# Four graph layers on one core: b2 added by DMA and bk on VectorE instead of matmuls, with a new order of work in layers 0 and 2

## The chip, the cores and the metric

The kernel runs on one core of a Trainium2 chip. The metric is the device time of one execution in microseconds, lower is better.

## The reference

The input is x, 64 graphs of 128 nodes with 256 features, and one 128 x 128 adjacency matrix per graph. Four layers follow one another, each inside a residual and a layer normalisation:

```
x = _layernorm(x + L0(x, adj, W1, b1, gamma, beta, W2, b2))   # hypergraph convolution, relu, layer norm, convolution + b2, + x
x = _layernorm(x + L1(x, adj, W_qk, W_v))                     # q k scores summed with adj, softmax over nodes, times v
x = _layernorm(x + L2(x, adj, Wv, bv, aw, ab, Wk, bk))        # attention transition T; relu(sum_k T^k x Wk[k] + bk[k])
x = _layernorm(x + L3(x, adj, w, a))                          # tanh attention, T x w
```

Layer 0 in full is `y = P norm(relu(P x W1 + b1)) W2 + b2`, with P = D^-1 H B^-1 H^T of the graph, and its result is `y + x`, so the layer normalisation sees `2 x + y`. In layer 2:

```
e = leaky_relu(sj[:, None, :] + si[:, :, None] + ab[0], negative_slope=0.2)
transition = A * exp(e); transition /= sum(transition, -1) + 1e-12
H = X Wk[0] + bk[0] + T X Wk[1] + bk[1] + T T X Wk[2] + bk[2];  return relu(H)
```

## The kernel before, in words

The 64 graphs are taken in 16 groups of four (`GP = 4`). x stays in SBUF (`K.x`, 64 KB a partition), and so does the transposed adjacency (`K.at`). Each layer has five programs, one an engine (SP, TensorE, ScalarE, VectorE, GpSimd), and each program is a function `step(g, p, has)` in which the order of the pieces is written out by hand. A step handles pieces of several groups at once: `has(-1)` means "if group g-1 exists", p is the parity of g. `over_layers` runs all steps of a layer on an engine and interleaves the last steps of one layer with the first of the next as the strings `SEAMS_*` say. Engines only meet through semaphores.

Precision is had by halves: a float32 value is split into an f16 high and an f16 low part, and `triple` makes three matmuls out of one product (L86 low x high, L87 high x low, L88 high x high).

Layer 0, per group on TensorE: `hidden` (four pieces, 1.3 us each), `spread_degrees`, `gram`, `mix_z` of the group before, `transpose_adj` and `degree` of a later group, `project` (four pieces), `mix_x`, `square_sums`. `mix_z` adds b2: a matmul of ones with `b2_parts` (L634) opens the bank, and P times zn (L635) is accumulated on it. `layer_out` on VectorE (L868) takes half of this plus x, loaded by SP into `K.x` (`load_resident`, L444). ScalarE makes relu, squares, z copies; GpSimd adds up the squares (`sum_squares`, L969), and `squares_high` (L698), `squares_low` and `square_sums` follow. During the first groups weights are prepared in parts of `K.x` and `K.at` that are not in use yet (`setup`); SP waits for them before it loads group 6.

Layer 2, per group on TensorE: `node_scores` (24 small matmuls), `project_near` (four pieces, six matmuls of 512 columns each), `spread_scores`, `project_far` (four), `walk_far` and `walk_mid` (four each, multiplications by T). `walk_mid` adds bk with a matmul of ones with `bk_parts` (L1546). ScalarE applies relu from PSUM (L1612) and VectorE adds x (L1665). The scores go: `logits` on ScalarE (L1587), leaky relu on VectorE (L1680), `exponentials` on ScalarE (L1619), `transition`, `row_sums` and `normalised` on VectorE, `T_high` and `T_low`, and two DMA transposes of T by SP.

x for a layer's matmuls has to be turned. `x_high` (ScalarE, L1114) and `x_low` (GpSimd, L1121) make halves of a group's x, and `transpose_x` (L1135, SP queue) turns them by DMA into `xT_hi` and `xT_lo`. There are two buffers of each, so the transposes of group g+2 overwrite those of group g. In layer 2 they wait for `near_ps` of group g, the fourth `project_near`:

```
if s == 0 and reused(g):
    sp.wait_ge(readers[0], upto(g - 2, readers[1], readers[1]))
sp.dma_start(F.xT[p][s][:].rearrange("p g d n -> p (g d) n"),
             F.xs[p][s].rearrange("p g d -> p (g d)"), transpose=True).then_inc(F.xT_in[p], 16)
```

and `node_scores(g+2)`, the first reader, waits for both (`transposed`).

## Time and profile before

| | |
|---|---|
| Median of 3 runs | 706.57 us (703.46 to 710.72) |
| Profiled execution, own time | 706.9 us |
| Its span | 704.9 us |
| Mean granted TensorE clock | 0.981 |
| Busy: TensorE, VectorE, ScalarE, GpSimd | 93%, 80%, 76%, 51% |
| Layer 0, 1, 2, 3, roughly | 0 to 285, to 390, to 600, to 705 us |

The span is what the profiler's records cover; the times of runs are a little longer. A line of a view names the source line, the engine, the operation and what it writes and reads. A matmul's duration contains its way through the array, so matmuls that follow each other overlap in the records: how long one holds the engine is seen from the start of the next.

### The profile page before, as it was taken

What the parts mean: (1) busy time and instruction counts of PE and PEld (TensorE: products, weight loads), DVE (VectorE), ACT (ScalarE), POOL (GpSimd) and SP (SyncE); (2) the same over time, 40 slices, a digit from 0 to 9 for tenths busy, and PEclk for the clock granted to TensorE, in tenths of its full rate; (3) what the DMA queues carried; (4) which work ended last, traced back from release to release, by engine and by line L of the source; (5) the groups of instructions that cost most, each with busy time, mean ns of one, the idle gap of its engine ahead of it and who ended that gap; (6) DMA issues with size and microseconds to landing.
All of it is one profiled execution on the core that took longest, in us unless ns stands there. A gap on an engine that the chain in (4) does not pass through costs nothing.

```text
span 704.9 us, 16982 instructions
## 1 busy us (share of the span) xinstructions
PE 652.6 (93%) x5526; PEld 469.1 (67%) x5526; DVE 560.8 (80%) x1746; ACT 538.7 (76%) x1193; POOL 358.3 (51%) x434
## 2 busy tenths in 40 slices
PE   5899999999999998989997899999989999899994
PEld 5667776777777775656664556666656766677783
DVE  4899899988888887588888668686867876688886
ACT  4768878787888878578887656777767776799996
POOL 2234455544444446466666324535335353688983
PEclk9999999999999999999999799999999999999998
DMA  9422324222222100476655133345533434377883
GB/s 280 148 74 84 98 65 131 75 77 75 76 76 76 62 16 16 94 157 134 134 133 117 44 81 78 87 87 91 92 74 78 90 77 75 61 169 175 180 189 129
DMA packets 168174, 71.50 MB, mean 101 GB/s; under 512 B 122260, under 2 KB 165654, under 8 KB 168088
## 3 DMA queue, kind: packets, MB, share of 16 engines
q1 hardware_dynamic: 166496, 70.41, 42.0%
q8 instruction: 45, 0.74, 0.4%
q14 instruction: 41, 0.34, 0.2%
q10 hardware_dynamic: 1592, 0.01, 0.1%
HBM read 28.46 MB, written 8.39 MB: 52 GB/s over the span
## 4 chain that ended last, share of the span: by engine, by line
PE 64%; DVE 10%; DMA 8%; POOL 7%; ACT 6%; issue 5%; SPq 1%; ACTq 0%; POOLq 0%; DVEq 0%
PE banks L86 17%; PE banks L88 16%; PE banks L87 16%; DMA xT_lo<-x_halves 7%; POOL x_halves L1121 4%; PE banks L635 3%; PE banks L594 3%; DVE l_st L1035 2%; ACT h_hi L683 2%; POOL l_rstd L1060 2%; PE banks L1440 1%; DVE l_pre L1312 1%; POOL l_U L1965 1%; PE banks L1546 1%; PE banks L580 1%
## 5 line engine op out<-in xcount | busy, mean ns | idle before, releaser
L1069 ACT ACTIVATE x_resident<-l_pre,l_nmr,l_rstd 128x256 f32<-128x256 f32 x256 | 141.0, 601 | 11.9 <-POOL l_nmr L1063 11.3
L969 POOL TENSOR_TENSOR hq<-hq 128x512 f32<-128x512 f32 x48 | 61.9, 1289 | 101.1 <-ACT hq L692 98.8
L1121 POOL TENSOR_TENSOR x_halves<-x_resident,x_halves 128x1024 f16<-128x1024 f32 x46 | 98.1, 2132 | 28.5 <-DVE l_pre L1312 24.1
L86 PE MATMUL banks<-Wk_lo,xT_hi 128*128 128x2 f16 (+2 forms) x384 | 95.1, 277 | 4.5 <-DMA xT_lo<-x_halves 4.5
L87 PE MATMUL banks<-Wk_hi,xT_lo 128*128 128x2 f16 (+2 forms) x384 | 96.0, 276 | 0.0
L88 PE MATMUL banks<-Wk_hi,xT_hi 128*128 128x2 f16 (+2 forms) x384 | 95.6, 275 | 0.0
L1035 DVE BATCH_NORM_STATS2 l_st<-l_pre 128x6 f32<-128x256 f32 x256 | 94.8, 414 | 0.0
L1060 POOL TENSOR_TENSOR l_rstd<-l_veps,minus_half 128x4 f32<-128x4 f32 x64 | 70.1, 1095 | 15.3 <-DVE l_veps L1049 11.9
L86 PE MATMUL banks<-W2T_lo,h_hi 128*128 128x257 f16 x256 | 70.9, 277 | 3.5 <-ACT zf L704 2.7
L1762 POOL TENSOR_TENSOR l_T_lo<-l_tf,l_T_hi 128x512 f16<-128x512 f32 x16 | 18.5, 1158 | 106.2 <-ACT l_T_hi L1606 106.2
L87 PE MATMUL banks<-W2T_hi,h_lo 128*128 128x257 f16 x256 | 70.9, 277 | 0.0
L88 PE MATMUL banks<-W2T_hi,h_hi 128*128 128x257 f16 x256 | 70.9, 277 | 0.0
L679 ACT ACTIVATE hf<-banks,b_col 128x512 f32<-128x512 f32 x64 | 43.9, 685 | 17.3 <-PE banks L88 16.9
L86 PE MATMUL banks<-xT_lo,W1T_hi 128*128 128x512 f16 x128 | 48.7, 380 | 2.9 <-DVE qkvT_lo L384 0.9
L86 PE MATMUL banks<-w_lo,xT_hi 128*128 128x1 f16 (+1 forms) x256 | 44.8, 218 | 6.1 <-DMA xT_lo<-x_halves 5.0
L86 PEld LDWEIGHTS banks<-Wk_lo,xT_hi 128*128 128x128 f16 x384 | 35.0, 98 | 21.2 <-DMA xT_lo<-x_halves 7.3
L88 PE MATMUL banks<-xT_hi,W1T_hi 128*128 128x512 f16 x128 | 48.5, 379 | 0.0
L87 PE MATMUL banks<-xT_hi,W1T_lo 128*128 128x512 f16 x128 | 48.5, 379 | 0.0
L1114 ACT ACTIVATE x_halves<-x_resident 128x1024 f16<-128x1024 f32 x46 | 48.4, 1052 | 0.0
L88 PEld LDWEIGHTS banks<-Wk_hi,xT_hi 128*128 128x128 f16 x384 | 35.4, 98 | 17.7 <-issue 1.4
L87 PE MATMUL banks<-w_hi,xT_lo 128*128 128x1 f16 (+1 forms) x256 | 45.8, 218 | 0.0
L88 PE MATMUL banks<-w_hi,xT_hi 128*128 128x1 f16 (+1 forms) x256 | 45.4, 218 | 0.0
(208 smaller groups left out, 1984.4 us busy)
## 6 DMA issues: line engine op xcount, KB each, us to landing
adj<-in_adj SPq DMA_DIRECT2D x32, 256.0 KB, 4.1
x_halves<-in_x SPq DMA_DIRECT2D x16, 512.0 KB, 3.9
x_resident<-in_x SPq DMA_DIRECT2D x16, 512.0 KB, 5.3
out<-x_resident SPq DMA_DIRECT2D x15, 512.0 KB, 3.3
l_adjT<-adjT_resident SPq DMA_DIRECT2D x16, 256.0 KB, 2.6
x_resident<-in_L_gnn_W SPq DMA_DIRECT2D x2, 512.0 KB, 5.6
x_resident<-in_L_gnn_Wk SPq DMA_DIRECT2D x1, 768.0 KB, 8.1
xT_hi<-x_halves SPq DMA_TRANSPOSE x48, 3.2
```

Source lines behind the costliest of these rows:

```text
L86: nc.tensor.matmul(out, lhs[0], rhs[1], start=start, stop=False, **kw)
L87: nc.tensor.matmul(out, lhs[1], rhs[0], start=False, stop=False, **kw)
L88: return nc.tensor.matmul(out, lhs[0], rhs[0], start=False, stop=stop, **kw)
L594: m = pe.matmul(b_mix[d][:, c], xst[p][:, j, d * 128:(d + 1) * 128], pf[p][:, c], start=True, stop=True)
L635: m = pe.matmul(o, pf[p][:, j * N:(j + 1) * N], zn[p][:, j, :], start=False, stop=True)
L679: act.activation(hf[:, h, :], b_hid[h % 2][:], ACT.Relu, bias=K.b1[:, h:h + 1], scale=1.0 / W_SCALE).then_inc(hf_ok, 1)
L969: pool.tensor_tensor(hq[:, 0, :], hq[:, 0, :], hq[:, h, :], ALU.add).then_inc(hqs_ok, 1)
L1035: dve.bn_stats(L.st[p][:, j, :], L.pre[p][:, j, :]).then_inc(L.st_ok, 1)
L1060: pool.tensor_tensor(L.rstd[p][:], L.veps[p][:], K.minus_half[:], ALU.pow).then_inc(L.rstd_ok, 1)
L1069: act.activation(K.x[:, gcols(g, j)], L.pre[p][:, j, :], ACT.Identity, bias=L.nmr[p][:, j:j + 1], scale=L.rstd[p][:, j:j + 1]).then_inc(L. ...
L1114: act.activation(F.xs[p][0], x_group(K, g), ACT.Copy).then_inc(F.x_hi, 1)
L1121: pool.tensor_tensor(F.xs[p][1], x_group(K, g), F.xs[p][0], ALU.subtract).then_inc(F.x_lo, 1)
```

## The change

Layer 0. b2 no longer goes through TensorE. b2 is loaded as a broadcast to all partitions, halved by ScalarE into `b2_half`; SP fills the part of `K.x` of two groups at a time with it (`fill_x`), and GpSimd issues a DMA that adds x onto it (`add_x`, `accum_op=ALU.add`), in place of `load_resident`. `mix_z` is one matmul a graph. `incidence` and `edge_weights` read the transposed adjacency in PSUM and not the copy in SBUF. The order of the steps on TensorE, ScalarE, VectorE and GpSimd is new in part.

Layer 2. The sum of the three bk is kept in float32 in all partitions (`bk_sum`), loaded by a broadcast DMA from the ACT queue. `walk_mid` has no bk matmul; VectorE scales the PSUM result and adds bk (`add_bk`), and the rectifier is the maximum in `residual`. Leaky relu is ScalarE's Prelu in `logits`; `exponentials` reads its result. The order on all engines is written anew (on SP and GpSimd with the same sequence of pieces as before, under other step numbers).

```
-                pe.matmul(o, K.ones16[:], K.b2row[:], start=True, stop=False)
-                m = pe.matmul(o, pf[p][:, j * N:(j + 1) * N], zn[p][:, j, :], start=False, stop=True)
+                m = pe.matmul(o, pf[p][:, j * N:(j + 1) * N], zn[p][:, j, :], start=True, stop=True)

+def fill_x(K, sp, pair):
+    cols = K.x[:, bass.ds(2 * pair * (GP * D), 2 * (GP * D))]
+    sp.dma_start(cols.rearrange("p (k d) -> p k d", d=D),
+                 K.b2half[:, None, :].to_broadcast([128, 2 * GP, D])).then_inc(K.filled[pair % 3], 16)

+        def add_x(g, p):
+            pool.wait_ge(K.filled[g // 2 % 3], 16 * (g // 6) + 16)
+            pool.dma_start(K.x[:, xcols(g)].rearrange("p (g d) -> p g d", g=GP),
+                           K.xd[:, bass.ds(g * GP, GP), :], accum_op=ALU.add).then_inc(K.x_in[p], 16)

-        act.wait_ge(const, 6)
-        for dst, src in rows:
-            act.dma_start(dst, src).then_inc(rows_in, 16)
+        act.dma_start(bkn, bk.rearrange("(a k) b -> a k b", a=1).to_broadcast([128, 3, D])).then_inc(rows_in, 16)

 layer 0, GpSimd step
             if has(2):
                 sum_squares(g + 2, 1)
+            if has(0):
+                next_x(g, p)
+            once(g, -2, add_x, 0, 0)
+            if has(2):
                 sum_squares(g + 2, 2)
                 sum_squares(g + 2, 3)

 layer 0, TensorE step
             if has(-1):
                 hidden(g - 1, q, 0)
+            if has(0):
+                spread_degrees(g, p)
+            if has(-1):
                 hidden(g - 1, q, 1)
                 hidden(g - 1, q, 2)
+            if has(-2):
+                mix_z(g - 2, p, 0)
+            if has(-1):
                 hidden(g - 1, q, 3)
-            if has(0):
-                spread_degrees(g, p)
+            if has(1):
+                transpose_adj(g + 1, q)
+            if has(0):
                 gram(g, p)
             if has(-2):
-                mix_z(g - 2, p, 0)
                 mix_z(g - 2, p, 1)

 layer 0, ScalarE step, end
             if has(0):
+                copy_z(g, 0)
                 squares_high(g)
-                copy_z(g, 0)

-            pe.matmul(o, K.ones16[:], K.bkrow[:], start=False, stop=False, skip_group_check=True)

 layer 2, TensorE step
             if has(-1):
+                walk_mid(g - 1, q, 1)
+                walk_mid(g - 1, q, 2)
+            if has(0):
+                project_far(g, p, 1)
+            if has(-1):
                 walk_mid(g - 1, q, 3)
             if has(1):
                 node_scores(nc, K, F, S, pe, g + 1, q, b_s, K.wk, D)
             if has(0):
                 project_near(g, p, 0)
+            if has(1):
+                spread_scores(nc, K, S, pe, g + 1, b_t, S.t_ok, GP)
+            if has(0):
                 project_near(g, p, 1)
-            if has(1):
-                spread_scores(nc, K, S, pe, g + 1, b_t, S.t_ok, GP)
-            if has(0):
                 project_far(g, p, 2)
+                project_near(g, p, 2)
                 project_far(g, p, 3)
-                project_near(g, p, 2)
+                walk_far(g, p, 0)
                 project_near(g, p, 3)
-                walk_far(g, p, 0)
                 walk_far(g, p, 1)
...
-            act.activation(S.t[:, j * N:(j + 1) * N], b_t[:, j * N:(j + 1) * N], ACT.Identity,
+            act.activation(S.t[:, j * N:(j + 1) * N], b_t[:, j * N:(j + 1) * N], ACT.Prelu, alpha=0.2,

 layer 2, ScalarE step, after the change
             logits(g + 1, 0); logits(g + 1, 1); logits(g + 1, 2)
             norm_apply(K, L, act, g - 2, p, 0 to 3)
             logits(g + 1, 3); far_high(g, 2); x_high(g + 2); far_high(g, 3)
             mid_high(g, 0 to 3); exponentials(g + 1); T_high(g + 1, q)
             far_high(g + 1, 0); far_high(g + 1, 1)

-            dve.tensor_tensor(L.pre[p][:, j, :], hr[:, j, :], K.x[:, gcols(g, j)],
-                              ALU.add).then_inc(L.pre_ok, 1)
+            dve.scalar_tensor_tensor(L.pre[p][:, j, :], hr[:, j, :], 0.0, K.x[:, gcols(g, j)], ALU.max,
+                                     ALU.add).then_inc(L.pre_ok, 1)

+        def add_bk(g, j):
...
+            dve.scalar_tensor_tensor(hr[:, j, :], b_near[j][:, D:2 * D], 1.0 / WK_SCALE, K.bk[:], ALU.mult,
+                                     ALU.add).then_inc(hr_ok, 1)

 layer 2, VectorE step, after the change
             residual(g - 1, 3); far_low(g, 1); norm_row(g - 1, 2 and 3); norm_variance(g - 1)
             far_low(g, 2); mid_low(g, 0); far_low(g, 3); mid_low(g, 1 and 2)
             add_bk(g, 0); mid_low(g, 3); residual(g, 0)
             transition(g + 1); row_sums(g + 1); add_bk(g, 1); normalised(g + 1)
             residual(g, 1); scores(g + 2); add_bk(g, 2 and 3); far_low(g + 1, 0)
             norm_row(g, 0 and 1); residual(g, 2)
```

## Rows read from the trace of the kernel before

**Rows 1.** Stretches: us, engines' busy us, granted clock, DMA share, GB/s.
```profile
0.00:20.00 20.00, 12.51 (x81) 11.00 (x82) 10.01 (x29) 8.15 (x17) 3.83 (x15) 1.00 0.96 288
...
60.00:220.00 160.00, 159.22 (x1342) 118.44 (x1340) 142.23 (x397) 129.34 (x250) 80.08 (x92) 1.00 0.26 79
420.00:583.00 163.00, 158.45 (x1408) 108.05 (x1407) 122.34 (x378) 118.75 (x300) 69.09 (x78) 1.00 0.43 84
```

**Rows 2.** Timeline of ScalarE in layer 0 (start, us, instruction, idle before): `dbc`, two groups.
```profile
143.49 0.60 ACT L711 ACTIVATE dbc<-banks 128x512 f32<-128x512 f32 x1 [0.33 <-PE banks L580]
...
159.90 0.60 ACT L711 ACTIVATE dbc<-banks 128x512 f32<-128x512 f32 x1 [0.33 <-PE banks L580]
```

**Rows 3.** Timeline of TensorE: start of layer 0, its steady period, its end.
```profile
8.11 1.94 PE L271 MATMUL banks<-ident,x_resident 128*128 128x128 f32 x8 [0.75 <-DMA x_resident<-in_L_gnn_W]
...
143.73 0.27 PE L634 MATMUL banks<-b_parts,ones 128*128 128x256 f16 x1
143.84 0.60 PE L635 MATMUL banks<-zn,P 128*128 128x256 f32 x2
...
156.21 0.38 PE L88 MATMUL banks<-xT_hi,W1T_hi 128*128 128x512 f16 x1
156.65 0.39 PE L86 MATMUL banks<-xT_lo,W1T_hi 128*128 128x512 f16 x1
...
281.18 0.28 PE L86 MATMUL banks<-W2T_lo,h_hi 128*128 128x257 f16 x1 [2.73 <-ACT zf L704]
```

**Rows 4.** Timelines of VectorE and GpSimd in layer 0.
```profile
6.23 0.43 DVE L791 TENSOR_SCALAR incT<-adjT_resident 128x512 f16<-128x512 f32 x1 [6.23 <-ACT adjT_resident L729]
...
148.64 0.73 DVE L791 TENSOR_SCALAR incT<-adjT_resident 128x512 f16<-128x512 f32 x1
...
144.68 1.27 POOL L969 TENSOR_TENSOR hq<-hq 128x512 f32<-128x512 f32 x1 [4.81 <-ACT hq L692]
146.35 2.74 POOL L969 TENSOR_TENSOR hq<-hq 128x512 f32<-128x512 f32 x2 [0.40 <-ACT hq L692]
```

**Rows 5.** Timeline of TensorE in layer 2, from one last `project_near` matmul to the next.
```profile
468.42 0.38 PE L88 MATMUL banks<-Wk_hi,xT_hi 128*128 128x512 f16 x1
...
470.21 0.27 PE L1546 MATMUL banks<-bk_parts,ones 128*128 128x256 f16 x1
...
473.35 0.18 PE L86 MATMUL banks<-Wk_lo,xT_hi 128*128 128x2 f16 x1
...
480.48 0.38 PE L87 MATMUL banks<-Wk_hi,xT_lo 128*128 128x512 f16 x1
480.69 0.38 PE L88 MATMUL banks<-Wk_hi,xT_hi 128*128 128x512 f16 x1
```

**Rows 6.** Timeline of the SP queue in layer 2: the two transposes of x.
```profile
468.88 1.23 SPq L1135 DMA_TRANSPOSE xT_hi<-x_halves  x1
470.15 1.33 SPq L1135 DMA_TRANSPOSE xT_lo<-x_halves  x1
```

**Rows 7.** Tile `xT_lo`, 440 to 590 us: landing; then waits, 420 to 583 us (total, times, longest).
```profile
DMA to landing us min/median/max: 3.1/3.2/4.8
...
PEld banks L86 <- DMA xT_lo<-x_halves: 5.5, 12, 1.9
```

**Rows 8.** Timeline of the SP queue in layer 0: the load of the resident x.
```profile
151.38 0.51 SPq L444 DMA_DIRECT2D x_resident<-in_x  x1
```

**Rows 9.** Timelines of ScalarE and GpSimd in layer 2: x's halves.
```profile
475.11 1.04 ACT L1114 ACTIVATE x_halves<-x_resident 128x1024 f16<-128x1024 f32 x1
...
479.09 2.12 POOL L1121 TENSOR_TENSOR x_halves<-x_resident,x_halves 128x1024 f16<-128x1024 f32 x1
```

**Rows 10.** Groups by shape (xcount | busy us, mean ns | idle before): ScalarE's, VectorE's.
```profile
L729 ACT ACT_TABLE_LOAD x1 | 1.3, 1283 | 4.3 <-issue 4.3
...
L1934 DVE SCALAR_TENSOR_TENSOR l_pre<-banks,l_rfac,x_resident 128x256 f32<-128x256 f32 x64 | 26.5, 478 | 0.6
...
L1680 DVE SCALAR_TENSOR_TENSOR l_lr<-l_t 128x512 f32<-128x512 f32 x16 | 14.1, 881 | 22.8 <-ACT l_t L1587 22.8
```

More of the change, by code:

```diff
@@ L733, in step @@
             if has(0):
+                mixed_high(g, p, 0)
                 mixed_high(g, p, 1)
@@ L779, in step @@
             if has(0):
+                copy_z(g, 0)
                 squares_high(g)
-                copy_z(g, 0)
-            if has(1):
-                mixed_high(g + 1, q, 0)
         return step, 2, 2
@@ L1496, in step @@
         def step(g, p, has):
[L1497 to L1498 removed]
+            q = 1 - p
             if has(2):
@@ L1630, in step @@
                 logits(g + 1, 2)
+            if has(-2):
+                norm_apply(K, L, act, g - 2, p, 0)
+                norm_apply(K, L, act, g - 2, p, 1)
+                norm_apply(K, L, act, g - 2, p, 2)
+                norm_apply(K, L, act, g - 2, p, 3)
+            if has(1):
                 logits(g + 1, 3)
@@ L1645, in step @@
                 mid_high(g, 3)
-            if has(-1):
-                norm_apply(K, L, act, g - 1, q, 3)
             if has(1):
+                exponentials(g + 1)
+                T_high(g + 1, q)
                 far_high(g + 1, 0)
-            if has(0):
-                relu(g, 0)
-                relu(g, 1)
-                relu(g, 2)
-                relu(g, 3)
-            if has(1):
                 far_high(g + 1, 1)
-        return step, 2, 1
+        return step, 2, 2
     def vector(dve):
@@ L1721, in step @@
             q = 1 - p
-            if has(1):
-                scores(g + 1)
             if has(-1):
                 residual(g - 1, q, 3)
-                norm_row(L, dve, g - 1, q, 2)
             if has(0):
-                far_low(g, 0)
                 far_low(g, 1)
             if has(-1):
+                norm_row(L, dve, g - 1, q, 2)
                 norm_row(L, dve, g - 1, q, 3)
                 norm_variance(L, dve, g - 1, q, EPS)
-            if has(1):
-                leaky(g + 1)
             if has(0):
                 far_low(g, 2)
+                mid_low(g, 0)
                 far_low(g, 3)
+                mid_low(g, 1)
+                mid_low(g, 2)
+                add_bk(g, 0)
+                mid_low(g, 3)
+                residual(g, p, 0)
             if has(1):
                 transition(g + 1, q)
-            if has(0):
-                mid_low(g, 0)
-                mid_low(g, 1)
-                mid_low(g, 2)
-                mid_low(g, 3)
-            if has(1):
                 row_sums(g + 1)
             if has(0):
-                residual(g, p, 0)
+                add_bk(g, 1)
+            if has(1):
+                normalised(g + 1)
+            if has(0):
                 residual(g, p, 1)
-                residual(g, p, 2)
+            if has(2):
+                scores(g + 2)
+            if has(0):
+                add_bk(g, 2)
+                add_bk(g, 3)
+            if has(1):
+                far_low(g + 1, 0)
+            if has(0):
                 norm_row(L, dve, g, p, 0)
                 norm_row(L, dve, g, p, 1)
-            if has(1):
-                normalised(g + 1)
-        return step, 1, 1
+                residual(g, p, 2)
+        return step, 2, 1
     def gpsimd(pool):
```

221 lines of the change are left out of this document (98 added, 123 removed).

## The prediction

> **What bounds the kernel now.** I read the engine shares first, then the table of stretches, the groups by cost, and then one period of layers 0 and 2 instruction by instruction. In the middle of layer 0 TensorE is busy 159.22 of 160 us at full granted clock [rows 1]. So layer 0 is a row of matmuls with nothing between them; VectorE beside it is busy 89% of that stretch and ScalarE 81%. The period there is the distance of two copies of `dbc`, 159.90 - 143.49 = 16.41 us [rows 2]. In layer 2 TensorE seems as full (158.45 of 163), but a busy share hides short waits, since each matmul is drawn with its tail. There the starts matter: the last matmul of `project_near` starts at 468.42 and, one group later, at 480.69 [rows 5], a period of 12.27 us.
>
> What sets these 12.27 us is a round that goes through a DMA. `transpose_x` for group g+2 overwrites the buffer of group g, so it waits for the fourth `project_near` of g. It starts at 468.88, its second transpose is issued at 470.15 [rows 6], and this takes 3.1 to 3.2 us to land [rows 7]. `node_scores(g+2)` stands behind it and starts at 473.35: 470.15 + 3.20. From there TensorE runs without a hole to the next last `project_near`, 480.69. The round is 4.93 us of turning and 7.34 us of matmuls, together the period. The wait view agrees: 12 waits of TensorE's weight loads for `xT_lo`, 5.5 us in all [rows 7]. TensorE's own work is 0.35 us a group shorter than the round. A matmul of 512 columns holds the engine 0.21 to 0.22 us (480.48 to 480.69 [rows 5]) and one of 256 columns 0.11 [rows 3]; 468.42 + 0.22 and twelve `walk_far` matmuls make 469.95, and the first bk matmul starts at 470.21; 28 matmuls on it would be 473.26, and `node_scores` starts at 473.35.
>
> **Layer 0, term by term.** Taken off TensorE: four b2 matmuls a group. Each one is drawn as 0.27 us, but the next starts 0.11 us later (143.73, 143.84 [rows 3]), so the engine gets 0.44 us back a group, not 1.1. The new order puts `spread_degrees` (0.45 us) between `hidden` 0 and 1; in the old one `hidden` 2 starts at 156.65 where it could start at 156.43, because ScalarE is still reading bank 0 [rows 3]. That 0.22 us goes too. 16.41 - 0.44 - 0.22 = 15.75 us.
>
> Can the others follow? I laid out one period with the durations of the profile. ScalarE ends the copy of z's second tile about 14.15 us after `hidden` 0 starts and `project` 3 wants it at 14.2: a wait of 0.0 to 0.3, I take 0.15. VectorE ends `degrees` at 16.05 and its next input comes at 16.16; its 14.6 us of work are 93% of 15.75, so it has about 0.1 us to spare at that spot and 0.6 us ahead of `hidden`. Incidence and edge weights read PSUM instead of the resident copy; the nearest rows (0.43 us with GpSimd idle, 0.73 us in the steady period [rows 4]) bound it by a gain of 0.3 and nothing, and I take nothing, since the steady row is the like one. I take -0.51 us a group, 15 groups: **-7.6 us**. Bounds: -9.9 (nothing waits) and 0 (VectorE or ScalarE takes over at 16.4).
>
> b2 now comes with x: SP fills pairs of groups with b2/2 (1 MB of writes a pair), and GpSimd adds x to it with a DMA (512 KB). This has three prices. (a) The landing. The slowest landing shown is 4.8 us [rows 7]; `add_x(g+2)` is issued about 14 us before `layer_out` wants it. Even at twice that time it hides. (b) SP: the fill takes the place of a 0.51 us issue [rows 8]; SP is idle nearly all of layer 0, and the loads behind it are a period early. Nothing. (c) The issue on GpSimd. The trace has none. It stands between `sum_squares` 1 and 2; behind it are queued `sum_squares` 2 and 3 (2.74 us together [rows 4]), then `squares_high` on ScalarE, `mixed_high` and the z copies, then `project` 3. By my layout `sum_squares` 1 ends at 8.4, ScalarE reaches `squares_high` at 12.2: 12.2 - 8.4 - 2.74 = 1.06 us are free; beyond that every us is a us of period. Bounds from the rows: 0.51 us (the same transfer issued by SP) and 2.13 us (GpSimd's longest instruction [rows 9]). I take 1.0, between them and near GpSimd's 1.27 us [rows 4], so nothing is added; at 2.13 it is +1.07 x 15 = +16 us.
>
> At the end of layer 0 TensorE waits 2.73 us for z's first tile [rows 3]; `copy_z` now stands ahead of `squares_high`, one ScalarE instruction of 512 columns (0.60 us for such a one [rows 2]): **-0.5**. At the start, bk as a broadcast brings 384 KB onto the ACT queue beside W1 and W2; at 288 GB/s [rows 1] that is 1.3 us, and TensorE waits for W at 8.11 [rows 3]. The two 512 KB resident loads that go stand behind W: **+1.0** (0 to 1.3). The sum of bk, the halving of b2 and the low halves are single instructions among idle ones: nothing.
>
> **Layer 2, term by term.** Off TensorE: four bk matmuls, 0.44 us a group. Off ScalarE, which isn't on the round: four rectifiers. The leaky step leaves VectorE (14.1 us in all, 0.88 a group [rows 10]), and Prelu on ScalarE replaces Identity with the same shape, so nothing is added there. VectorE gets four `add_bk` from PSUM and SBUF; the nearest row is L1934, 26.5 us for 64, 0.41 us each: 1.66 us a group; `residual` keeps its shape. Net +0.8 us on 9.2 us a group (122.34 of 163 us [rows 1]), 10.0 of some 12.6: 79%.
>
> Now the round. The bk matmuls stand in the part where TensorE waits for the turning anyway (between `project_near` 3 and `node_scores`). Taking them out makes that wait longer, not the period shorter. The wait for `mid_low` (0.26 us) lies there too. What does change the round is the order: `walk_far` 0 (three matmuls, 0.33 us) moves ahead of `project_near` 3. `transpose_x` still waits for `project_near` 3, so these 0.33 us enter the round: 4.93 + 7.34 + 0.33 = 12.60. TensorE then waits 1.1 us a group for `xT_lo`. Spread scores, one `project_near` earlier, are inside the round either way. Over 15 groups: **+5.0 us**. Two other rounds come near: x's halves by ScalarE (1.04), low halves by GpSimd (2.12 [rows 9]), transpose, scores, spread, three logits, four `norm_apply`, which the new order puts ahead of the next x halves: which my layout of one period puts at 12.65; and exponentials, `transition`, row sums, T, second logits, which gives 12.3 to 12.6. Neither is far above, both could add 0.1 to 0.5.
>
> In the first group of layer 2 nothing hides the leaky step: **-0.9**.
>
> **Sum**, against the profiled execution's own 706.9 us (span 704.9; the median of the three runs is 706.57): -7.6 - 0.5 + 1.0 + 5.0 - 0.9 = -3.0, so 703.9, said as 704.
>
> **Rivals.**
> (1) Layer 2 follows TensorE's work: the turning lands earlier or is asked for earlier, and the removed matmuls and the wait count. Then -0.79 us a group, -11.9 instead of +5.0: 687. For it: the waits for `xT_lo` differ, 1.9 us at most and 0.5 on average [rows 7], so the round may not bind every group. Against it: 473.35 is 3.20 us behind the issue, within the landing times, and no line changes what `transpose_x` waits for. 0.24.
> (2) Slower: the DMA issue on GpSimd takes longer than the 1.06 us that are free. It decides from there on: at 1.7 us it costs 0.64 x 15 = 9.6 us and gives 714, at 2.13 us 720. For it: GpSimd and VectorE hinder one another here, as `incT` shows with 0.43 us beside an idle GpSimd and 0.73 beside a busy one [rows 4], so 0.7 us on top of an issue of 1.0 us is what one blocking VectorE instruction adds. Against it: GpSimd waits 4.81 us for ScalarE before its sums [rows 4], so it is there in time. The Trainium skill, SBUF — State Buffer, section "SBUF: two separate sides", speaks against such a DMA: descriptors of a DMA issued from GpSimd are written by GpSimd, and VectorE's two-port instructions lock it out. No row here shows such a DMA. 0.18.
> (3) VectorE or ScalarE becomes the bound, in layer 0 (the 7.6 us are not had) or in layer 2 (+0.5 us a group): 712. 0.12.
> (4) Prelu and Exp don't share a table: two loads of 1283 ns [rows 10] a group, some of it on the second round: +20 to +40, about 735. The one load of the trace serves Relu, Square, Tanh, Exp and Identity. The Trainium skill, ScalarE: Activation LUTs, section "Table sets: the hidden batching unit", puts cheap functions into every set, but names no Prelu there; by it this rival falls away, and the one load agrees. 0.02.
>
> **How the numbers follow.** The forecast holds 0.44, with its own range 698 to 711. The range reaches from rival 1 (687, its upper part, as start and order effects soften it: 689) to rival 2's end, 720. 1% (7 us) is about what a measurement of this kernel can tell from no change. Faster by more than that (below 699.5): rival 1 and 0.06 of the forecast, 0.30. Slower (above 713.6): most of rival 2 (0.14), half of rival 3 (0.06), rival 4, and 0.04 of the forecast, 0.26. Same: 0.44.
>
> **What would show it.** The starts of the last `project_near` matmul in layer 2 lie 12.6 us apart, and the wait for `xT_lo` before `node_scores` is about 1.1 us a group instead of 0.4; with rival 1 they lie 11.5 to 11.8 apart. Copies of `dbc` lie 15.9 us apart in layer 0; with rival 2 more, with `squares_high` late behind `hq` and GpSimd's DMA issue longer than 1.06 us. No second table load. Wrong would be, first of all, the layout by hand where it leaves 0.1 us of slack.

## The result

| | before | after |
|---|---|---|
| Median (runs) | 706.6 us (4, 703.5 to 710.7) | 716.2 us (4, 713.0 to 720.2) |
| Profiled execution, own time and span | 706.9, 704.9 us | 720.2, 718.2 us |
| Mean granted clock | 0.981 | 0.972 |
| First and last start of `T_high` in layer 2 | 398.4, 588.3 us | 398.5, 601.1 us |

The ratio is 1.0136, with a 95% interval of 1.0086 to 1.0187: the changed kernel is slower by 1.4%. The forecast was 704 us with "within 1%" as the likeliest; the time lies inside its range (689 to 720) and outside the likeliest case's own (698 to 711). Ratios here and below are over executions in the faster of two states that the kernel runs in; the medians of e8, e13, e14 and e15 contain one or two slower ones. The profiled execution of the changed kernel is the slowest of its four, so its loss against the profiled one before, 13.3 us, is more than the 9.6 us between the medians.

The last row of the table says where: until layer 2 begins nothing is won or lost, and layer 2 takes 202.6 us between its first and last `T_high` where it took 189.9. The stretches of the changed kernel, same columns as [rows 1]:

```profile
0.00:20.00 20.00, 11.96 (x72) 10.93 (x73) 9.04 (x25) 8.56 (x18) 3.23 (x13) 0.91 0.94 280
60.00:220.00 160.00, 157.91 (x1307) 120.46 (x1304) 139.93 (x403) 128.81 (x254) 93.29 (x102) 1.00 0.50 114
420.00:583.00 163.00, 143.05 (x1226) 95.60 (x1224) 118.83 (x380) 89.63 (x224) 58.14 (x72) 0.96 0.40 77
```

In layer 2 TensorE's busy time fell from 158.45 to 143.05 us and its clock from 1.00 to 0.96. Every engine has more idle time than before: nobody's work is the bound, a round of waits is. Here is that round in the timelines of TensorE and of the SP queue, as in [rows 5, 6]:

```profile
526.28 0.38 PE L88 MATMUL banks<-Wk_hi,xT_hi 128*128 128x512 f16 x1
...
531.20 0.18 PE L86 MATMUL banks<-Wk_lo,xT_hi 128*128 128x2 f16 x1 [0.94 <-DMA xT_lo<-x_halves]
...
538.87 0.38 PE L88 MATMUL banks<-Wk_hi,xT_hi 128*128 128x512 f16 x1
```
```profile
526.73 1.25 SPq L1144 DMA_TRANSPOSE xT_hi<-x_halves  x1
528.03 1.33 SPq L1144 DMA_TRANSPOSE xT_lo<-x_halves  x1
```

From the last `project_near` matmul to `node_scores` it is 4.92 us (4.93 before), from there to the next last `project_near` 7.67 us (7.34 before, plus `walk_far` 0's 0.33). The period is 12.59 us, forecast 12.60. TensorE idles 0.94 us in each round. The wait view of 420 to 583 us and the landing, against [rows 7]:

```profile
PEld banks L86 <- DMA xT_lo<-x_halves: 23.3, 12, 3.4
PE banks L86 <- DMA xT_lo<-x_halves: 19.9, 12, 3.2
```
```profile
DMA to landing us min/median/max: 3.1/3.2/5.4
```

The first two rows are TensorE's weight loads (PEld) and its matmuls (PE); the matmuls' row counts here. Twelve waits are 19.9 us, not 12 x 0.94 = 11.3, and the longest is 3.2 us. That is the part that the forecast missed. The distances between `T_high` starts (from the trace, us):

```
before  11.55 15.49 12.31 12.27 12.29 12.23 12.27 12.25 12.28 13.63 14.36 12.17 12.27 12.26 12.24
after   11.65 12.61 12.59 12.62 15.45 16.49 14.28 12.61 12.57 12.56 12.58 12.79 15.47 15.83 12.57
```

Five groups of the changed kernel take 1.7 to 3.9 us more than its 12.6, 14.5 us in all; three of the kernel before exceed its 12.27, by 6.7 us in all. So the 12.7 us are 15 x 0.33 = 4.9 of steady loss and 7.8 of late groups.

What a late group looks like, from the table of stretches (a usual group, then the end of the round before the first late one, then what follows) and TensorE's timeline:

```profile
431.00:443.60 12.60, 11.63 (x106) 7.95 (x105) 10.00 (x33) 7.56 (x20) 4.87 (x7) 1.00 0.40 83
443.60:448.60 5.00, 2.71 (x25) 2.18 (x23) 4.53 (x12) 1.69 (x5) 0.13 (x1) 1.00 0.98 108
448.60:453.90 5.30, 5.23 (x46) 2.86 (x47) 4.28 (x17) 1.74 (x6) 1.55 (x3) 0.68 0.41 99
```
```profile
448.67 0.18 PE L86 MATMUL banks<-Wk_lo,xT_hi 128*128 128x2 f16 x1 [2.36 <-DMA xT_lo<-x_halves]
...
450.12 0.63 PE L88 MATMUL banks<-Wk_hi,xT_hi 128*128 128x512 f16 x1
450.55 0.63 PE L86 MATMUL banks<-Wk_lo,xT_hi 128*128 128x512 f16 x1
```

The low transpose was issued at 444.06 and landed 4.6 us later, TensorE idled 2.36 us, and its clock then fell from 2.4 to 1.2 GHz for 3.4 us: matmuls of 512 columns start 0.43 us apart instead of 0.21. The group is 2.85 us late, 1.4 by the landing and the rest by the clock and what waits behind it. Over the five late groups the landings are 8.4 us over the usual 3.2 in sum, and the clock, which fell in four of them, with what follows makes the other 6.1. (The third, where it stayed up, is 1.68 us late, as much as its landing of 4.8 us.) In the kernel before three landings were as late (4.5 to 4.8 us), but there TensorE came to `node_scores` together with the data in a usual group, so it idled only 1.3 to 1.6 us; the clock fell once, at the start of the layer, and stayed up in the other two.

Why did that landing take 4.6 us? The DMA view of the two stretches from the issue to `node_scores`, the late one and then a usual one:

```profile
q1 hardware_dynamic: 2065, 0.51, 101.9%
q8 instruction: 1, 0.02, 2.1%
```
```profile
q1 hardware_dynamic: 2049, 0.51, 85.0%
```

The same 0.51 MB, and beside them one transfer of instructions: 16 KB, 1.53 us long. Some twenty packets of 256 B, which usually take 0.02 us, took 1.4 to 1.8 us beside it. Other late landings look different: at 568.86 no packet of 256 B took over 0.13 us and the last one ended 2.7 us after the issue, as usual, but the last packet of 4 B, which usually ends with them, ended at 3.55 us, when the instruction transfer beside it (2.63 to 3.53 us) was through. The instruction transfers come every 1.17 groups on average, so their place in the round wanders, and late groups come in clusters.

Layer 0, steady period: `dbc` on ScalarE, then GpSimd with its new DMA issue:

```profile
144.59 0.59 ACT L709 ACTIVATE dbc<-banks 128x512 f32<-128x512 f32 x1
160.67 0.59 ACT L709 ACTIVATE dbc<-banks 128x512 f32<-128x512 f32 x1
```
```profile
163.01 1.32 POOL L973 TENSOR_TENSOR hq<-hq 128x512 f32<-128x512 f32 x1 [5.18 <-ACT hq L690]
164.28 1.32 POOL L952 DMA_DIRECT2D x_resident<-in_x  x1
165.14 1.77 POOL L973 TENSOR_TENSOR hq<-hq 128x512 f32<-128x512 f32 x1
```
```profile
ACT hqs_hi L696 <- POOL hq L973: 5.2, 10, 0.5
PEld banks L86 <- ACT zf L702: 2.3, 10, 0.2
```

The period is 16.08 us: less than 16.41 [rows 2], more than the forecast 15.90. In this view of 60 to 220 us (total, times, longest) `squares_high` waits 0.5 us for GpSimd in every group (not at all before), and TensorE 0.2 us for z. Only one table load of ScalarE is there, as before.

### The profile page after: what moved, and what is told of

Same layout as the page of the kernel before. It is cut to its first block, busy times and chain, and to the rows that moved or that the text cites. A ratio compares the mean times of both kernels' runs of the same rounds, so it can differ in the third digit from the quotient of the medians.

```text
span 718.2 us, 16696 instructions
## 1 busy us (share of the span) xinstructions
PE 645.3 (90%) x5398; PEld 468.5 (65%) x5398; DVE 566.1 (79%) x1792; ACT 509.2 (71%) x1127; POOL 373.2 (52%) x448
## 4 chain that ended last, share of the span: by engine, by line
PE 30%; DMA 13%; POOL 7%; DVE 6%; issue 3%; SPq 2%; ACT 2%; ACTq 0%; POOLq 0%; DVEq 0%
DMA xT_lo<-x_halves 13%; PE banks L86 9%; PE banks L88 9%; PE banks L87 8%; POOL x_halves L1130 4%; SPq L1144 2%; DVE l_st L1044 2%; PE banks L1450 2%; POOL l_rstd L1069 1%; POOL l_U L1966 1%; DVE l_pre L1321 1%; PE banks L1234 1%; PE banks L1246 1%; PE banks L1837 1%; ACT x_resident L1078 0%
## 5 line engine op out<-in xcount | busy, mean ns | idle before, releaser
L1078 ACT ACTIVATE x_resident<-l_pre,l_nmr,l_rstd 128x256 f32<-128x256 f32 x256 | 138.2, 609 | 8.8 <-POOL l_nmr L1072 8.2
L973 POOL TENSOR_TENSOR hq<-hq 128x512 f32<-128x512 f32 x48 | 69.4, 1446 | 95.7 <-ACT hq L690 93.4
L1044 DVE BATCH_NORM_STATS2 l_st<-l_pre 128x6 f32<-128x256 f32 x256 | 90.7, 411 | 0.0
L839 DVE TENSOR_TENSOR h_lo<-hf,h_hi 128x512 f16<-128x512 f32 x64 | 42.8, 690 | 12.1 <-issue 8.2
L1715 DVE TENSOR_TENSOR l_mid_lo<-banks,l_mid_hi 128x256 f16<-128x256 f32 x64 | 25.5, 420 | 28.8 <-ACT l_mid_hi L1609 28.8
```

What stands on the lines that cost most here:

```text
L839: dve.tensor_tensor(hs[1][:, h, :], hf[:, h, :], hs[0][:, h, :], ALU.subtract).then_inc(h_lo, 1)
L973: pool.tensor_tensor(hq[:, 0, :], hq[:, 0, :], hq[:, h, :], ALU.add).then_inc(hqs_ok, 1)
L1044: dve.bn_stats(L.st[p][:, j, :], L.pre[p][:, j, :]).then_inc(L.st_ok, 1)
L1078: act.activation(K.x[:, gcols(g, j)], L.pre[p][:, j, :], ACT.Identity, bias=L.nmr[p][:, j:j + 1], scale=L.rstd[p][:, j:j + 1]).then_inc(L. ...
L1715: dve.tensor_tensor(mid[j][1][:], b_near[j][:, 0:D], mid[j][0][:], ALU.subtract).then_inc(mid_lo, 1)
```

## The experiments

Each was timed beside the kernel before, whose median was 706.6 to 709.1 us from one set to the next; compare by the ratio to it. The changed kernel's is 1.0136. All distances are from the traces, us. Landings are those of `xT_lo` for the second to the fifteenth group of layer 2. A ratio is from 5 to 12 executions (4 for the changed kernel), the distances and landings are from the one that was profiled.

| run | ratio (95%) | layer 0, steady | layer 2, steady | late landings (over 3.8 us, of 14) |
|---|---|---|---|---|
| e1 near 3 first | 1.014 (1.008 to 1.020) | 16.08 | 12.76 | 1 |
| e2 start order | 1.016 (1.010 to 1.022) | 16.09 | 12.6 | 4 |
| e3 issue last | 1.019 (1.014 to 1.025) | 15.78 | 12.6 | 6 |
| e4 before, no bk | 1.005 (1.001 to 1.009) | 16.41 | 12.2 | 4 |
| e5 before, walk first | 1.018 (1.012 to 1.023) | 16.41 | 12.2 to 13.4 | 6 |
| e6 early halves | 1.029 (1.024 to 1.033) | 16.08 | 13.78 | 1 |
| e7 split transposes | 1.027 (1.022 to 1.032) | 16.08 | 13.78 | halves: 2.5, three of them 4.3 |
| e8 filled | 1.006 (1.003 to 1.010) | 16.08 | 12.6 | 3 |
| e9 layer 0 alone | 0.998 (0.995 to 1.001) | 16.08 | 12.27 | 5 |
| e10 layer 0 mended | 1.010 (1.007 to 1.013) | 15.78 | 12.2 | 6 |
| e11 mended, filled | 1.016 (1.013 to 1.019) | 15.78 | 12.6 | 4 |
| e12 fetch away | 1.001 (0.998 to 1.004) | 16.07 | 12.57 | 1 |
| e13 fetch on | 1.013 (1.008 to 1.019) | 16.08 | 12.6 | 4 |
| e14 mended | 1.000 (0.997 to 1.004) | 15.78 | 12.27 | 6 |
| e15 adds in idle | 0.998 (0.994 to 1.001) | 15.78 | 12.27 | 6 |
| e16 all mended | 1.000 (0.997 to 1.003) | 15.78 | 12.57 | 1 |

### Which half of the change costs

**e9**: the changed kernel with `layer2` of the kernel before (bk's matmuls, rectifiers, leaky step and order).

> Half of the change: the changed kernel's layer 0, with the kernel before's layer 2 (its bk matmuls, rectifiers, leaky step and order; bk's two half-precision rows are made from the sum that VectorE would use). Theory A (the whole loss lies in layer 2, and layer 0 as changed gains nothing by the start of layer 2): T_high starts at about 398.5 us as in both kernels, 12.27 us apart, and the time is 706 to 708, that of the kernel before. Theory B (layer 0's shorter period does count): 703 or lower. Theory C (layer 0 loses as well): 710 or more.

706.5 us, first `T_high` at 397.4, 12.27 apart. Theory A: layer 0 as changed gives nothing, and the whole loss is layer 2's.

### The steady loss in layer 2

**e4**, in the kernel before:

```
-            pe.matmul(o, K.ones16[:], K.bkrow[:], start=False, stop=False, skip_group_check=True)
```

> The kernel before with only the four bk matmuls a group of layer 2 taken out (bk is left out of the computation). Theory A (they stand in TensorE's wait for the transposes, so they cost nothing): T_high starts stay 12.27 us apart, the wait for xT_lo before node_scores grows by 0.44 us, and the time is that of the kernel before, 706 to 707 us. Theory B (TensorE's work sets layer 2): 11.83 us apart, 7 us lower, 700 us.

708.8 us, without bk in the result. The usual groups keep 12.2 to 12.3 us and TensorE's wait before `node_scores` is 0.39 us where there was none:

```profile
436.82 0.18 PE L86 MATMUL banks<-Wk_lo,xT_hi 128*128 128x2 f16 x1 [0.39 <-DMA xT_lo<-x_halves]
449.05 0.18 PE L86 MATMUL banks<-Wk_lo,xT_hi 128*128 128x2 f16 x1 [0.39 <-DMA xT_lo<-x_halves]
```

Taking 64 matmuls out of layer 2 brought nothing, as forecast for bk; the kernel is 0.5% slower, with four late landings where the kernel before has three.

**e1**, in the changed kernel, and **e5**, the reverse edit in the kernel before:

```
                 project_far(g, p, 3)
-                walk_far(g, p, 0)
                 project_near(g, p, 3)
+                walk_far(g, p, 0)
```

> The changed kernel with one edit of layer 2's TensorE order undone: project_near 3 stands ahead of walk_far 0 again. Theory A (walk_far 0 in the round of the transposes costs 0.33 us a group): the starts of T_high lie 12.27 us apart instead of 12.60, which is -5 us, and since TensorE then idles 0.7 us a group less than 1.1 before node_scores, late landings cost less as well: 704 to 711 us where the changed kernel has 716. Theory B (the loss of layer 2 comes from the new VectorE and ScalarE order or from late landings alone): 12.6 us apart as before the edit and 716 us.

> The kernel before with one edit: in layer 2 walk_far 0 stands ahead of project_near 3, as in the changed kernel. Theory A (near 3 to transposes to node_scores is the round that sets 12.27 us, and walk_far 0 lengthens it): T_high starts lie 12.60 us apart, 712 us or a little more, where the kernel before has 707. Theory B (another round sets it): 12.27 us apart and 707.

Both missed. In e1 the period is 12.76, not 12.27. Its SP timeline shows why:

```profile
495.75 1.23 SPq L1144 DMA_TRANSPOSE xT_hi<-x_halves  x1
497.36 1.24 SPq L1144 DMA_TRANSPOSE xT_lo<-x_halves  x1
```

The low transpose is issued 1.61 us behind the high one, not 1.28: GpSimd's low half ends at 497.34. So the low half now holds up the transpose. With the first round shortened, the second one (x halves, low half, transpose, scores, spread, logits, `norm_apply`) binds; the forecast had it at 12.65. So the changed kernel stands between two rounds of nearly one length. That `walk_far` 0 makes the first one longer is shown by its own timeline (7.67 us instead of 7.34); undoing this one edit doesn't give the 0.33 us back, because the second round is no shorter. No run gave the 0.33 us back in the changed kernel, so their share in the loss rests on the timeline. In e5 the usual groups are 12.2 to 13.4 us apart, most of them more than the 12.60 of the sum: `walk_far` 0 also meets the turned T earlier, and TensorE waits for it ("0.33 <-DMA l_TT_lo" ahead of it at 498.22) and for `mid_hi`. Six late groups come on top; the 12 us of e5 are a loss from this edit, but not 0.33 x 15.

**e6** and **e7** moved both x halves ahead (with e1's edit, `project_near` 3 ahead of `walk_far` 0), and e7 also cut each transpose in two. On ScalarE and GpSimd, in both:

```
+            if halves_due(F, g + 2):
+                x_high(K, F, L, act, g + 2, p)
             if has(1):
                 logits(g + 1, 0)
...
-            if halves_due(F, g):
-                x_low(K, F, pool, g, p)
-            if has(-1):
-                T_low(g - 1, q)
-            if has(-2):
-                norm_scales(K, L, pool, g - 2, p)
+            if has(-2):
+                T_low(g - 2, p)
+            if halves_due(F, g):
+                x_low(K, F, pool, g, p)
+            if has(-3):
+                norm_scales(K, L, pool, g - 3, q)
```

and e7 besides, with the waits of its readers counted for it:

```
+    for half in range(2):
+        js = slice(2 * half, 2 * half + 2)
...
+                sp.wait_ge(readers[0], upto(g - 2, readers[1], 2 * half + 2))
+            sp.dma_start(F.xT[p][s][:, js].rearrange("p g d n -> p (g d) n"), ...
```

> The changed kernel, in layer 2: project_near 3 ahead of walk_far 0, x_high first in ScalarE's step, and x_low ahead of norm_scales on GpSimd, so that both x halves are there 2 us before the transposes want them. Theory A (the 12.76 us of the run with near 3 first come from a second round, x_high to x_low to the low transpose to node_scores): with it broken the first round is left, 12.27 us, 8 us less than the changed kernel's 716 by the steady groups alone, down to 704 if fewer clock drops come with it. Theory B (12.76 us come from VectorE's new order): 12.6 to 12.8 us still, 714.

> As the run with early halves, and each transpose of x in layer 2 is cut in two DMAs: graphs 0 and 1 once project_near 1 is through, graphs 2 and 3 after project_near 3. Theory A (layer 2 waits for the landing): 0.7 us or more leave the round, TensorE's work of 11.66 us sets the period, 11.6 to 11.8 us, and the time is 716 - 14 = 702 us or lower, 694 if the clock drops go too; TensorE no longer waits for xT_lo. Theory B (VectorE's or ScalarE's order sets 12.3 us or more): 12.3 us and more, 708 or above.

Both missed, with 13.78 us a group: a wait took the place of the one removed. VectorE and GpSimd in e6:

```profile
498.72 2.35 DVE L1658 SCALAR_TENSOR_TENSOR l_pre<-l_hr,x_resident 128x256 f32<-128x256 f32 x1
```
```profile
498.65 2.13 POOL L1130 TENSOR_TENSOR x_halves<-x_resident,x_halves 128x1024 f16<-128x1024 f32 x1 [0.33 <-ACT x_halves L1123]
```

`residual`, 0.41 us in every other place (406 to 421 ns over 48 of them in the changed kernel), takes 2.35 us when it meets `x_low`: VectorE, with two operands in SBUF, stands until GpSimd's instruction is through (498.72 + 2.35 = 501.07, 0.3 us behind its end). `far_low` 2 and `project_far` follow late. The Trainium skill, SBUF — State Buffer, section "SBUF: two separate sides", says that a VectorE operation with two SBUF inputs and a GpSimd operation that reads SBUF exclude each other for the whole instruction. The rows agree, 2.35 us against 0.41.

### The late groups

**e8**: zeros added to the bank, twice ahead of each `walk_mid`, so that TensorE has 0.88 us more to do a group and never a changed result.

```
+            for _ in range(2):
+                pe.matmul(o, K.ones16[:], K.zeros16[:], start=False, stop=False, skip_group_check=True)
```

> The changed kernel with eight more matmuls a group in layer 2: each walk_mid adds ones times zero twice to its bank before its own three, 0.88 us of TensorE a group in the stretch between project_near 3 and node_scores. The result is the same. Theory A (that stretch is TensorE waiting for a landing, and a TensorE that idles too long there loses its clock afterwards): steady groups stay at 12.6 us, the wait before node_scores falls from 1.1 to 0.2 us, there are fewer or no half-clock stretches in layer 2, and the kernel with more work is faster, 710 to 712 us. Theory B (TensorE's work counts): 13.5 us a group, 716 + 13 = 729.

711.2 us: the kernel with 128 more matmuls is 5 us faster (0.7% by the ratios). Its steady groups stay at 12.6, TensorE's waits in 420 to 583 us fall from 19.9 to 4.4 us, the clock there is 1.00:

```profile
420.00:583.00 163.00, 158.11 (x1422) 110.25 (x1421) 129.13 (x409) 95.46 (x240) 60.49 (x76) 1.00 0.43 82
```

Landings are still late in three groups (up to 4.7 us), but they cost 0.7 to 1.5 us each without the clock. Idle time of TensorE was not free. Not all of the gain is the clock's, though: the added instructions also moved the instruction transfers, and three landings are late instead of five.

**e12** and **e13** test where the landings' lateness comes from. Both replace e8's filling by 18 matmuls of one column; e13 has 23 more, once.

```
e12  +            for _ in range(4 + j % 2):
e13  +            for _ in range(4 + j % 2 + (23 if is_first(g) and j == 0 else 0)):
     +                pe.matmul(o[:, 0:1], K.ones16[:], K.zeros16[:, 0:1], start=False, stop=False, ...)
```

> The changed kernel with 18 more matmuls of one column a group in layer 2 (ones times zero added to the bank before each walk_mid's own three; the result is the same), some 0.5 us of TensorE a group in its wait before node_scores. The trace of the changed kernel has one instruction transfer of 16 KB in TensorE's queue per 1.16 groups (256 instructions at 219.5 a group), so its place in the group wanders, and the slow landings of xT_lo (4.6 to 5.4 us) are those with such a transfer under way. With 36 instructions more a group it is one transfer a group, at one place. Theory A (these transfers make the landings late): they stay near the start of T_high, all landings of xT_lo take 3.2 us, T_high starts are 12.6 us apart in every group but the first, and the time is 14 us lower by the profile, 6 to 10 by the medians: 706 to 710. Theory B (the landings are late for another reason): three to five slow ones still, 713 or above.

> The run before this one with 23 more matmuls of one column in the first group of layer 2 alone (0.6 us once). They move the instruction transfer by 46 instructions, 0.18 of a group, onto the landing of xT_lo, and it stays there. Theory A (instruction transfers make the landings late, and the longer wait costs TensorE its clock): most groups have a slow landing of 4.5 us or more and lie 14 to 16 us apart: 725 to 750 us from 0.6 us of work. Theory B: as the run before.

The Trainium skill, Runtime: NRT & Kernel Launch, section "Instruction fetch mechanics", says that instructions are fetched in blocks of 16 KiB, 256 of them, and that this is mostly hidden. The size agrees with the trace, and so does the count: transfers came 1.17 groups apart, 1.09 with e8's 8 matmuls (and their weight loads) more, and 1.00 with 18 more. That it is hidden doesn't agree.

In e12 the transfers stay at the start of `T_high` and one landing of 14 is late, by 0.7 us, beside a transfer of another queue. The distances behind the first are 12.56 to 12.84 with one of 13.29, and the time is 707.8 us: 1.3% less than the changed kernel with 0.5 us a group more to do. The added matmuls fill TensorE's wait in part as well, so it is the pair of e12 and e13, filled alike, that sets the transfers apart. The stretch of 420 to 583 us in both:

```profile
420.00:583.00 163.00, 155.69 (x1567) 107.88 (x1566) 128.96 (x413) 97.50 (x245) 63.41 (x78) 1.00 0.41 83
```
```profile
420.00:583.00 163.00, 150.70 (x1497) 104.16 (x1494) 123.50 (x392) 91.23 (x229) 58.70 (x72) 0.98 0.40 82
```
In e13 the transfers begin 2.5 to 3.3 us after the issue of the low transpose, at the edge of its landing. Four of the 14 landings are late there (4.0 to 4.7 us; one of them beside another queue's transfer, as in e12), the rest are not, and the ratio is back at 1.013. I had aimed at the middle and expected most of them late; the shift was too small. Still, 0.6 us of work in one group took the whole gain away. Over 17 traces (the two kernels' and all experiments' but e7, whose transposes are cut) there are 238 such landings: 66 took over 3.8 us, and in each of these an instruction transfer, of TensorE's queue or another's, was under way between 1.0 and 3.2 us after the issue; in the 172 others it was so 48 times. In no trace was a landing late without the transfer, and the transfer alone is not enough. In 37 of the 66 some packets of 256 B took over 1 us; in 18 they ended early and a closing packet of 4 B ended with the instruction transfer, 0.3 us or more behind them.

### Layer 0

**e3**: GpSimd's issue behind the sums.

```
-            if has(0):
-                next_x(g, p)
             once(g, -2, add_x, 0, 0)
             if has(2):
                 sum_squares(g + 2, 2)
                 sum_squares(g + 2, 3)
+            if has(0):
+                next_x(g, p)
```

> The changed kernel with GpSimd's DMA issue moved behind sum_squares 2 and 3. Theory A (the issue, 0.86 us from its start to the next sum, makes squares_high wait 0.5 us and project 3 wait 0.3 us a group): dbc copies lie 15.8 us apart instead of 16.08 in layer 0, squares_high no longer waits for GpSimd, and the time is 4 us lower, 712. Theory B (another chain, VectorE's or ScalarE's own work, sets 16.08 us): 16.08 as it was, and 716 us.

`dbc` copies lie 15.78 us apart as expected (the forecast's sum of TensorE's work was 15.75), and neither wait is left. The time did not fall (718.5 us): six groups of layer 2 were late in the profiled run, and its `T_high` starts span 205.6 us.

**e2**: `turn_qkv` behind `mix_x` and `products` 0 behind `operator` again, as before the change.

```
-            once(g, 1, W.turn_qkv, pe)
...
                 mix_x(g, p, 1)
+            once(g, 1, W.turn_qkv, pe)
...
-            once(g, 0, W.products, dve, 0)
             if has(1):
                 operator(g + 1, q)
+            once(g, 0, W.products, dve, 0)
```

> The changed kernel with two one-time pieces put back where they stood in the kernel before: turn_qkv behind mix_x on TensorE, products 0 behind operator on VectorE. Theory A (TensorE's waits of 1.52 us at 30.7 and 1.78 us at 36.0 come from this order): the third distance of two dbc copies is 17.4 us instead of 19.36, and the time is 2 us lower, 714. Theory B (the startup is late because of the new transfers, bk's broadcast and b2's fill): the distance stays at 19.4 and the time at 716.

Missed: third distance 19.20 us (the way to the first `dbc` is counted as the first distance, so the third lies between the second copy and the third). TensorE's waits only moved elsewhere. **e10** put this order together with all DMA issues of GpSimd behind the sums (on e9's kernel, as e14 and e15):

```
                 sum_squares(g + 2, 3)
+            if has(0):
+                next_x(g, p)
+            once(g, -1, add_x, 0, 0)
+            once(g, -1, add_x, 1, 1)
```

> As the run with layer 0 alone, and in layer 0 all of GpSimd's DMA issues stand behind the sums of squares, turn_qkv behind mix_x and products 0 behind operator. Theory A (the issues delay GpSimd's sums in the first groups as they do in the steady ones, and the once-only pieces hold TensorE up): the third distance of dbc copies is 17.4 to 18 us instead of 19.2 to 19.4, the steady one 15.78, L0 ends 5 us sooner and the time is 701 to 703, below both kernels. Theory B (the transfers themselves are late at the start, or the end of layer 0 takes back what its middle gains): 705 to 707.

The third distance is 17.60, but the fourth 28.2: the first transfer now came a step too late, and VectorE waited 10.6 us for it. 715.7 us, by my misplacement. **e11**, the same layer 0 with e8's filling:

> The changed kernel with layer 0 mended as in the run before and eight matmuls of ones times zero a group in layer 2 as in the run with filling. Theory A (the two effects add): 711 - 4 = 707 us, with 12.6 us a group in layer 2. Theory B (layer 0's gain is taken back at its end): 711.

719 us with the same hole (27.2 us); nothing follows from its time. **e14** has the first two issues in their own step, behind its sums, **e15** one step later, behind `squares_low`, where GpSimd has nothing to do:

```
e14               sum_squares(g + 2, 3)
     ...
     +            once(g, -2, add_x, 0, 0)
                  once(g, -2, add_x, 1, 1)
e15               squares_low(g + 1)
     +            once(g, -1, add_x, 0, 0)
     +            once(g, -1, add_x, 1, 1)
```

> The kernel before's layer 2 with the changed kernel's layer 0 in which GpSimd's DMA issues stand behind the sums of squares of the same step (also the first two, which in the earlier mended run came a step too late), turn_qkv behind mix_x and products 0 behind operator. Theory A: the third distance of dbc copies is 17.6 us, the fourth 16.5 instead of 28.2, the steady ones 15.78, and the time is 3 to 5 us below that of layer 0 alone (706.5): 702 to 704. Theory B (the end of layer 0 takes it back, since VectorE and ScalarE set its last two groups): 706.

> The kernel before's layer 2 with the changed kernel's layer 0 as in the second mended run, but GpSimd issues its first two DMAs one step later, right behind squares_low, where it has 4 us of nothing. Theory A (VectorE's once-only products, which read two SBUF operands, run only when GpSimd is between its own instructions, so that two DMA issues of 0.9 us behind the sums hold up VectorE and then TensorE): the third distance of dbc copies is 17.6 us instead of 19.5, the products' four instructions take 4.0 us in all instead of 5.9, and the time is 2 us below that of the second mended run, 704 to 706. Theory B (the two transfers themselves, 1 MB of DMA, make the start late): 19.5 us and 707.6.

Third distance 19.50 and 17.60 us, from the place of two issues alone. The products (four instructions) in e14 and e15, and GpSimd in the changed kernel, whose issues stand among the first group's sums:

```profile
L400 DVE TENSOR_TENSOR x_resident<-adjT_resident x4: 891/1424/2328, 31.9 to 37.0; 128x256 f32<-128x256 f32 x4
```
```profile
L400 DVE TENSOR_TENSOR x_resident<-adjT_resident x4: 415/1134/1485, 30.2 to 34.4; 128x256 f32<-128x256 f32 x4
```
```profile
30.83 1.47 POOL L952 DMA_DIRECT2D x_resident<-in_x  x1
```

Around this last line stand sums at 29.55 and 31.83 and a second issue at 34.96. VectorE's products, two SBUF operands each and 0.41 us when alone, are held until GpSimd is between instructions, and `P` or `wcol_lo` behind them holds up TensorE. The four durations add up to 3.2 us in the kernel before, 5.8 in the changed one, 6.1 in e14 and 4.2 in e15. It is the mechanism of e6 in another layer. e15 ends layer 0 4 us sooner than the changed kernel and is 704.6 us, not told apart from the kernel before.

**e16** puts e15's layer 0 before e12's layer 2.

> The changed kernel with layer 0 as in the run before this one and layer 2 as in the run with the instruction transfers moved away. Theory A (the effects add): third distance 17.6 us, steady distance 15.78 in layer 0, 12.57 in layer 2 with no slow landing but the one or two near another queue's instruction transfer; 707.8 - 1.9 - 2.4 = 703 to 704 us, some 0.6% below the kernel before. Theory B (layer 0's gain is taken back at its end): 707 to 708.

Layer 0's last `dbc` starts at 251.7 us (257.1 in the changed kernel), layer 2's groups are 12.57 apart with one late, and the time is 705.4, ratio 1.000. Layer 1 gave the gain back: its 16 exponentials span 95.3 us where they spanned 91.4 in the changed kernel, with distances of 8.3 and 8.2 instead of 7.1 and 6.4. The runs that share the changed kernel's layers 0 and 1 (e1, e6, e7, e8, e12, e13) have 92.0 to 93.5 there, so some of it comes and goes without any edit of these layers. What takes it was not tested. No version beats the kernel before by more than the measurement can tell.

## Why the prediction was wrong

**Layer 2's round: right.** 12.60 forecast, 12.59 in the timeline, by the terms named; bk's matmuls bought nothing (e4), and rival 1 (layer 2 follows TensorE's work, 0.24) is out. That `walk_far` 0 alone is the 0.33 us is read from the timeline; e1 and e5, which were to show it, both missed. The 1.1 us of waiting is 0.94. VectorE's load (118.8 us of 163), ScalarE's and the tables (one load) are as forecast, and rivals 3 and 4 fall. Rival 4 falls by the one table load of the trace alone; what the prediction put beside it does not name Prelu and could not settle it.

**The step that failed: what the wait costs.** The prediction put TensorE's idle 1.1 us a group down as free, because the period stays the same. It saw the landing's range, 3.1 to 4.8 us [rows 7], and used the median. In the kernel before, TensorE arrived with the data, so a landing 1.4 us late cost 1.4 us. In the changed kernel the same lateness comes on top of 0.94 us of idleness; TensorE then often loses its clock, which makes the round later still. This term was put at nothing: it is 7.8 us in the profiled run, and by an estimate from the medians (9.6 - 13.3 + 7.8) about 4 us in the usual one. e8 (idle filled, 5 us gained) and e12 against e13 (cause of lateness moved away, 8 to 9 us gained by the ratio) show it from two sides, though neither edit changes one thing alone: e8 has fewer late landings too. How often landings are late depends on where instruction transfers fall, which no row cited ahead of the prediction showed.

**Layer 0: mis-sized, three times.** The forecast was -7.1 us with its start and end; nothing was left by layer 2.
- The steady period fell by 0.33 us, not 0.51: 16.08 us instead of the forecast's 15.90. TensorE's sum was right (15.75, and 15.78 in e3). The slack behind GpSimd was put at 1.06 us; the issue and what it adds to the sums make these 0.93 us longer (5.35 from the first sum to `squares_high`, 4.42 in e3), and `squares_high` waits 0.52, so the slack was 0.4. Rival 2's mechanism was real, at 0.3 us a group (16.08 against 15.78 in e3), where the end of its range has 1.07.
- Only nine of the 15 distances are at 16.08, the last seven among them. Of those in which weights are prepared four are 16.4 to 16.6 (16.4 to 16.7 before); the hand layout was of a group without them.
- The start costs more than the 1.0 us that bk's broadcast was given. The third distance is 19.36 instead of 17.36, and `dbc` itself now stands 1.5 us earlier in its group than the work around it (the square sums of the last steady group start at 267.8 us before and 268.1 after, though the last `dbc` is 1.2 us earlier), so the start lost 3.7 us. Two issues on GpSimd and VectorE's products explain 1.9 of them (e14, e15).

**The end of layer 0 and the first group of layer 2**: TensorE's last wait is 2.54 us instead of 2.73, so -0.2 instead of -0.5; the first distance of layer 2 is 11.65 and not shorter, so the -0.9 did not come.

With the terms as measured: start +3.7, layer 0 -3.4, layer 2 steady +4.9, late groups +7.8, together +13.0; the spans differ by 13.3. These are terms of the two profiled executions.

## What to carry to other kernels

An engine that waits in a round is not at rest for free: find what happens to the round when its slowest transfer comes at its longest, not its median, and whether TensorE's idle time before it is long enough to cost the clock. Where TensorE must wait for a DMA each round, cheap matmuls of zeros in that wait can be worth more than the matmuls that were removed. An instruction of VectorE with two SBUF operands may be placed only where GpSimd is idle, and a GpSimd DMA issue counts as work of GpSimd.

## What the runs showed of the hardware

- TensorE's instructions come by DMA, 16 KB every 12 to 19 us in layer 2 of the two kernels, 0.9 to 1.6 us long, and some 256 B packets beside one took up to 1.9 us instead of 0.02. The two transposes of x, 2048 packets, landed late when one of these was slow, and also when only a last packet of 4 B ended behind the instruction transfer (568.86 in the changed kernel: 3.55 us instead of 2.7). With one such block a group the place of the collision stood still, clear of the landing (e12) or at its edge (e13).
- A residual addition of 0.41 us took 2.35 us beside a GpSimd instruction of 2.13 (e6).
- A DMA issued by GpSimd holds its queue for 0.8 to 1.0 us (start to the next start: 164.28 to 165.14), though its line is drawn with 1.3 to 1.5 us.
- With a wait for `xT_lo` TensorE's clock fell to 1.2 GHz for 3.4 us (twice 6.8) in some rounds of layer 2 and not in others, during the wait or within 2 us behind it: in 8 of 13 rounds with a wait over 2.3 us, and in 10 of 34 with one of 1.2 to 2.3 us (all 18 traces).
